# A two-layer graph network on one core: a wait, a GpSimd start and the last output block of the convolution are rearranged

## The reference

```python
src, dst = add_self_loops(edge_index, n)
h   = relu(gcn_conv(x1, W1, b1, src, dst, n))
out = gcn_conv(h, W2, b2, src, dst, n)
# gcn_conv(x, W, b): h = x @ W; dinv = 1/sqrt(deg); scatter-add of h[src]*dinv[src]*dinv[dst]; + b
return layernorm(x1 + out)      # (x - mean) / sqrt(var + 1e-5) over the 768 features
```

## Time and profile before

| | us |
|---|---|
| runs (median of 3) | 1649.15 |
| the profiled execution's own time | 1648.01 |
| its span in the profile | 1646.2 |
| TensorE busy in the span | 1624.3 |
| VectorE busy | 1222.6 |
| ScalarE busy | 761.0 |
| GpSimd busy | 217.7 |

### The profile page before, as it was taken

The page is one execution under the profiler, slowest core; times in us unless marked ns, Lnnn a source line. Parts: engine busy times, 40 slices in busy tenths (PEclk is TensorE's granted clock), DMA queues, the critical chain, the costliest instruction groups (busy, mean ns, idle before and its releaser), DMA issues. The chain is left out here.

```text
span 1646.2 us, 21875 instructions
## 1 busy us (share of the span) xinstructions
PE 1624.3 (99%) x7528; PEld 1360.4 (83%) x7528; DVE 1222.6 (74%) x2429; ACT 761.0 (46%) x1218; POOL 217.7 (13%) x145
## 2 busy tenths in 40 slices
PE   9999999999999999999999999999999998999998
PEld 6778888888878888888888888888888887989898
DVE  7778657655988778778777787887786668785447
ACT  3222223322565565556555555655565435644340
POOL 3112132222200000000000000000000001023003
PEclk9999999999999999999999999999999999999999
DMA  7444555984647475557647575865654447023222
GB/s 285 142 154 155 166 188 191 230 223 154 218 162 193 175 218 157 130 190 227 131 176 201 156 167 189 201 151 165 193 151 178 163 167 197 21 90 96 66 94 91
DMA packets 135396, 271.86 MB, mean 165 GB/s; under 512 B 24299, under 2 KB 83573, under 8 KB 122741
## 3 DMA queue, kind: packets, MB, share of 16 engines
q1 hardware_dynamic: 133844, 267.16, 53.6%
q0 software_dynamic: 1152, 3.15, 1.0%
q10 hardware_dynamic: 288, 0.13, 0.0%
HBM read 210.01 MB, written 60.40 MB: 164 GB/s over the span
## 5 line engine op out<-in xcount | busy, mean ns | idle before, releaser
L41 PE MATMUL psum<-ph,hc 128*128 128x512 f32 x768 | 299.3, 390 | 2.2 <-DVE pl L1079 1.2
L42 PE MATMUL psum<-pl,hc 128*128 128x512 f32 x768 | 298.8, 389 | 0.0
L43 PE MATMUL psum<-ph,hc 128*128 128x512 f32 x768 | 298.8, 389 | 0.0
L41 PE MATMUL psum<-wh,xTh 128*128 128x512 f32 x570 | 226.9, 398 | 0.7 <-issue 0.7
L42 PE MATMUL psum<-wl,xTh 128*128 128x512 f32 x570 | 222.4, 390 | 0.0
L43 PE MATMUL psum<-wh,xTl 128*128 128x512 f32 x570 | 222.3, 390 | 0.0
L1018 DVE CUSTOM_DVE_ANT_0 junk<-psum,a_bc 128x512 bf16<-128x512 f32 (+1 forms) x256 | 129.9, 554 | 115.7 <-ACT st L666 105.5
L666 ACT CAST st<-psum 128x512 fp32r<-128x512 f32 x96 | 56.4, 588 | 290.2 <-PE psum L43 287.4
L739 ACT ACTIVATE he<-mean,bias 128x512 f32<-128x512 f32 x96 | 69.6, 725 | 237.2 <-DVE mean L1167 237.2
L41 PEld LDWEIGHTS psum<-ph,hc 128*128 128x128 f32 x768 | 144.1, 188 | 33.9 <-DVE pl L1079 2.1
L43 PEld LDWEIGHTS psum<-ph,hc 128*128 128x128 f32 x768 | 144.1, 188 | 29.9
(11 more groups left out here) (292 smaller groups left out, 3162.0 us busy)
## 6 DMA issues: line engine op xcount, KB each, us to landing
hc<-h_scratch SPq DMA_DIRECT2D x96, 1024.0 KB, 6.1
h_scratch<-st SPq DMA_DIRECT2D x96, 512.0 KB, 3.2
w2r<-in_L_gnn_W SPq DMA_DIRECT2D x96, 384.0 KB, 7.0
wr<-in_L_gnn_W SPq DMA_DIRECT2D x11, 1536.0 KB, 9.1
gwr<-in_L_gnn_W SPq DMA_DIRECT2D x24, 384.0 KB, 3.4
row_bc<-logits_scratch SPq DMA_DIRECT2D x16, 512.0 KB, 13.7
expo_bc<-expo_scratch SPq DMA_DIRECT2D x16, 512.0 KB, 6.3
a_bc<-in_L_gnn_a_src SPq DMA_DIRECT2D x12, 256.0 KB, 7.0
```

The costliest lines, as they stand in the source:

```text
L41: nc.tensor.matmul(out, sh, mh, start=first, stop=False, skip_group_check=not grouped)
L42: nc.tensor.matmul(out, sh, ml, start=False, stop=False, skip_group_check=not grouped)
L43: return nc.tensor.matmul(out, sl, mh, start=False, stop=last, skip_group_check=not grouped)
```

## The change

1. TensorE: in the first group, the wait for `sx_lo` is left out at the last row block (b = 7), and stands instead ahead of the four low products of line 2120.
2. GpSimd: the counts of half 0 begin when `y_lo` has reached 6 (all low parts of the first product made), instead of when `sx_lo` has reached 8.
3. The last output block is split as 512 and 256 columns instead of 384 and 384, in TensorE's products, the additions and the stores. It is measured in three pieces of 256 columns. VectorE scales the 512 columns, ScalarE the 256 (`x * root + (-mean * root)`); for this VectorE writes the negated mean, and ScalarE multiplies it by the root.
4. Four more semaphores of the early part are cleared by GpSimd and used again.

```diff
-    early_sems = [edges_in, key_int, key_made, keyT_full, span_done, touch_full]
+    early_sems = [edges_in, key_int, key_made, keyT_full, span_done, touch_full, low_out, key_out, cols_full, cols_done]
...
+    END_PARTS = ((0, CW), (CW, D))
...
-        pool.wait_ge(sx_lo, NB)
+        pool.wait_ge(y_lo, FB)
...
-            act.wait_ge(norm_step, NORM_STEPS * n + NORM_ROOT)
+            act.wait_ge(norm_step, NORM_STEPS * n + (NORM_ROOT if n < NB - 1 else END_ROOT))
...
+        b, (lo, hi) = HNB - 1, END_PARTS[1]
+        act.wait_ge(norm_step, NORM_STEPS * (NB - 1) + END_ROOT + 2)
+        nc.scalar.activation(end_shift[:, 1:2], end_shift[:, 0:1], ACT.Copy, scale=root[:, b:b + 1]).then_inc(root_done, 1)
+        act.wait_ge(root_done, NB + 1)
+        nc.scalar.activation(x1[:, b, lo:hi], x1[:, b, lo:hi], ACT.Identity, bias=end_shift[:, 1:2], scale=root[:, b:b + 1]).then_inc(end_done[1], 1)
...
+            for j in range(lo // 256, hi // 256):
+                nc.vector.bn_stats(end_stats[:, j, :], x1[:, b, j * 256:(j + 1) * 256]).then_inc(norm_step, 1)
...
+        nc.vector.tensor_scalar(end_shift[:, 0:1], moments[:, b, 0:1], -1.0, None, ALU.mult).then_inc(norm_step, 1)
...
-        for i in range(2):
-            cs = slice(i * HC, (i + 1) * HC)
-            nc.vector.tensor_scalar(x1[:, b, cs], x1[:, b, cs], moments[:, b, 0:1], root[:, b:b + 1], ALU.subtract, ALU.mult).then_inc(norm_step, 1)
+        lo, hi = END_PARTS[0]
+        nc.vector.tensor_scalar(x1[:, b, lo:hi], x1[:, b, lo:hi], moments[:, b, 0:1], root[:, b:b + 1], ALU.subtract, ALU.mult).then_inc(end_done[0], 1)
...
                     pe.wait_ge(sx_hi, b + 1)
-                    pe.wait_ge(sx_lo, b + 1)
+                    if b < NB - 1:
+                        pe.wait_ge(sx_lo, b + 1)
...
+            pe.wait_ge(sx_lo, NB)
             for f in group:
                 nc.tensor.matmul(banks[f][:, :], xl[:, NB - 1, f * P:(f + 1) * P], ch[:, NB - 1, :], start=False, stop=True,
...
-                cs = slice(i * HC, (i + 1) * HC)
+                lo, hi = END_PARTS[i] if n == NB - 1 else (i * HC, (i + 1) * HC)
+                cs = slice(lo, hi)
```

More of the change, by code:

```diff
@@ L1801, in _ @@
             conv_tensor(pe, many_linked)
-NORM_STEPS, NORM_ROOT = 6, 4
+NORM_STEPS, NORM_ROOT, END_ROOT = 6, 4, 5
 def normalise(nc, dve, row, stats, moments, root, n, added, step, root_done):
@@ L1868, in graph_convolution @@
     root = put("groot", 100608, [P, NB], F32)
+    end_stats = put("gend_stats", 100640, [P, 3, 6], F32)
+    end_shift = put("gend_shift", 100736, [P, 2], F32)
+    END_PARTS = ((0, CW), (CW, D))
     ch2 = put("gch2", 102464, [P, NB, HALF], F32R)
@@ L1883, in graph_convolution @@
     agg_full, added, norm_step, root_done, out_done = (spare.pop() for _ in range(5))
+    end_done = [spare.pop() for _ in range(2)]
     CH = 2 * FB
@@ L1926, in sync @@
         b = HNB - 1
-        for i in range(2):
-            cs = slice(i * HC, (i + 1) * HC)
-            sp.wait_ge(norm_step, NORM_STEPS * NB + i)
-            sp.dma_start(out[b * P:(b + 1) * P, cs], x1[:, b, cs]).then_inc(out_done, 16)
+        for i, (lo, hi) in enumerate(END_PARTS):
+            sp.wait_ge(end_done[i], 1)
+            sp.dma_start(out[b * P:(b + 1) * P, lo:hi], x1[:, b, lo:hi]).then_inc(out_done, 16)
         sp.wait_ge(out_done, 16 * (NB + 1))
     def gpsimd(pool):
-        pool.wait_ge(sx_lo, NB)
+        pool.wait_ge(y_lo, FB)
         pool.wait_ge(ch_hi, NB)
@@ L2079, in vector @@
         dve.wait_ge(xb, NB)
-        for i in range(2):
-            cs = slice(i * HC, (i + 1) * HC)
+        for i, (lo, hi) in enumerate(END_PARTS):
             dve.wait_ge(agg_full, NB + i)
-            nc.vector.scalar_tensor_tensor(out=x1[:, b, cs], in0=banks[2 * (n % 4) + i][:, 0:HC], scalar=dinv[:, b:b + 1], in1=x1[:, b, cs],
+            nc.vector.scalar_tensor_tensor(out=x1[:, b, lo:hi], in0=banks[2 * (n % 4) + i][:, 0:hi - lo], scalar=dinv[:, b:b + 1], in1=x1[:, b, lo:hi],
                                            op0=ALU.mult, op1=ALU.add).then_inc(added, 1)
             dve.wait_ge(added, 2 * n + i + 1)
-            nc.vector.bn_stats(stats[:, b, i, :], x1[:, b, cs]).then_inc(norm_step, 1)
-        dve.wait_ge(norm_step, at + 2)
-        nc.vector.bn_aggr(moments[:, b, :], stats[:, b, :, :].rearrange("p i s -> p (i s)")).then_inc(norm_step, 1)
+            for j in range(lo // 256, hi // 256):
+                nc.vector.bn_stats(end_stats[:, j, :], x1[:, b, j * 256:(j + 1) * 256]).then_inc(norm_step, 1)
         dve.wait_ge(norm_step, at + 3)
+        nc.vector.bn_aggr(moments[:, b, :], end_stats[:, :, :].rearrange("p i s -> p (i s)")).then_inc(norm_step, 1)
+        dve.wait_ge(norm_step, at + 4)
         nc.vector.tensor_scalar(root[:, b:b + 1], moments[:, b, 1:2], LN_EPS, None, ALU.add).then_inc(norm_step, 1)
+        nc.vector.tensor_scalar(end_shift[:, 0:1], moments[:, b, 0:1], -1.0, None, ALU.mult).then_inc(norm_step, 1)
         dve.wait_ge(root_done, n + 1)
         nc.vector.reciprocal(root[:, b:b + 1], root[:, b:b + 1]).then_inc(norm_step, 1)
-        dve.wait_ge(norm_step, at + 5)
-        for i in range(2):
-            cs = slice(i * HC, (i + 1) * HC)
-            nc.vector.tensor_scalar(x1[:, b, cs], x1[:, b, cs], moments[:, b, 0:1], root[:, b:b + 1], ALU.subtract, ALU.mult).then_inc(norm_step, 1)
+        dve.wait_ge(norm_step, at + END_ROOT + 2)
+        lo, hi = END_PARTS[0]
+        nc.vector.tensor_scalar(x1[:, b, lo:hi], x1[:, b, lo:hi], moments[:, b, 0:1], root[:, b:b + 1], ALU.subtract, ALU.mult).then_inc(end_done[0], 1)
     def tensor(pe, many):
@@ L2198, in tensor @@
                         pe.wait_ge(rows_hi, s + 1 if s < HNB else HNB + 2 * (s - HNB) + 2)
-                    nc.tensor.matmul(bank[:, 0:HC], high[:, s, bs], xh[:, s, cs], start=(s == 0), stop=False)
+                    nc.tensor.matmul(bank[:, 0:hi - lo], high[:, s, bs], xh[:, s, cs], start=(s == 0), stop=False)
                 with pe.If(many > 0):
@@ L2202, in tensor @@
                     for s in range(NB):
-                        nc.tensor.matmul(bank[:, 0:HC], low[:, s, bs], xh[:, s, cs], start=False, stop=False)
+                        nc.tensor.matmul(bank[:, 0:hi - lo], low[:, s, bs], xh[:, s, cs], start=False, stop=False)
                 for s in range(NB):
@@ L2206, in tensor @@
                         pe.wait_ge(rows_lo, s + 1 if s < HNB else HNB + 2 * (s - HNB) + 2)
-                    last = nc.tensor.matmul(bank[:, 0:HC], high[:, s, bs], xl[:, s, cs], start=False, stop=(s == NB - 1))
+                    last = nc.tensor.matmul(bank[:, 0:hi - lo], high[:, s, bs], xl[:, s, cs], start=False, stop=(s == NB - 1))
                 if n == NB - 1 and i == 0:
```

## The result

Nine runs of the changed kernel have a median of 1653.49 us, nine of the kernel before 1649.15: ratio 1.0027, 95% interval 1.0018 to 1.0035. The change made the kernel slower by 4.3 us (0.26%). That is above the 0.2% that I had called no change, though the interval reaches down to 0.18%, and it is just outside the range. The profiled execution is the fastest of the nine (1651.35 us); its span is 1649.6 us, 3.4 more than before.

What follows compares the result with a forecast made beforehand. TensorE, busy 1624.3 of 1646.2 us, was taken as the bound; +2.1 us from the stall less 0.2 at the end gave +1.9, so 1649.9 for one execution and a median of 1651.0 us, range 1646.8 to 1653.2.

Steps and rivals of the forecast that it cites:

- What follows in PE's order is dense, and takes the delay over in full: TensorE after its stall for chunk 10: the delay of 2.1 us against before is kept whole.
- Rival A: GpSimd's counts keep their 24.26 us, `c0_lo` at 1507.8, TensorE +4.3 us, total 1653.2 us; chance 0.12.
- Part 1: Moved `sx_lo` wait at block 7: high products start before `sxl` is done, putting TensorE 0.97 us earlier.
- Part 2, the start: With GpSimd idle, VectorE is not slowed, so TensorE's step k = 1 starts 1.65 us sooner (bounds 1.5 and 1.8).
- The gap of 7 us moves with the first subtraction: GpSimd's 7.01 us of issue after its first cast belongs to the first subtraction and moves later with it.
- Rival B: No stall, because the 7.01 us gap does not move or GpSimd runs clean: 1647.3 us; chance 0.18.
- `c0_lo` at 1505.65: GpSimd's counts complete at 1505.65: first subtraction at 1483.57 plus 17.1 us of blocks and 5.0 us of slowing.
- The stall: TensorE waits 3.8 us for weight chunk 10, ready at 1518.0, and stands 2.1 us later than before.
- point of decision: `c0_lo` at 1501.9: each us the counts finish beyond it costs TensorE one us.
- Part 3: Last output block as 512 and 256 columns: TensorE's time unchanged, the end 0.2 us earlier (bounds 0 and 0.4).
- rival C: In the last block, 256 columns cost TensorE as much as 384, ending it 0.85 us later: 1651.9 us; chance 0.05.
- The median: Whole kernel: runs' median lies 1.14 us above the profiled-like execution's 1649.9, so 1651.0 us, +0.12%.

Runs made afterwards that it cites:

- e7: Changed kernel plus 28 extra TensorE products of 128 columns just before its wait for weight chunk 10 (result invalid, timing only): 1652.00 us, ratio 1.0022.
- e3: Kernel before with only TensorE's wait on the last `sxl` moved behind the high products, ahead of the low ones: 1647.85 us, ratio 0.9995.
- e5: Changed kernel, but ScalarE and VectorE make weight chunks 10 and 11 before the counts of half 1: 1646.31 us, ratio 0.9984.
- e6: Changed kernel plus one extra GpSimd subtraction of 128 columns at the counts' old starting point: 1645.71 us, ratio 0.9983.
- e1: Changed kernel, but GpSimd's counts start where they did before, at the last `sxl`: 1648.01 us, ratio 0.9995.
- e2: Kernel before with only GpSimd's counts started later, at `y_lo` 6: 1654.83 us, ratio 1.0033.
- e8: Changed kernel, but GpSimd's counts start at `y_lo` 3 instead of 6: 1646.49 us, ratio 0.9985.

## Why the prediction was wrong

**The step that failed** is "What follows in PE's order is dense, and takes the delay over in full". Dense it is, but not at the same speed: behind a stall of 4.5 us the clock was granted at half level for over 3 us (10 products of 0.32 us instead of 0.174, and what lies around them: 1.7 us by the yardstick, 1.4 to 1.6 by e7's profile). I had worked out a stall of 3.8 us and never asked what an idle TensorE costs when it is over. The prediction put this at nothing without a reason. In the convolution before, TensorE ran at 1.00 with no idle time above the 0.87 us of the earlier trace rows; but the same trace, at its start, had a row that shows the cost, and I did not look there. TensorE idles 2.94 us, the clock is then at 0.50, and products of 512 columns start 0.43 us apart (46.23, 46.66, 47.09) instead of 0.23. Timeline of PE, then windows, of the kernel before:
```profile
43.92 1.03 PE L1541 MATMUL psum<-hot_key,hot_low 128*128 128x256 bf16 x4 [2.94 <-issue]
...
46.66 0.63 PE L43 MATMUL psum<-wh,xTl 128*128 128x512 f32 x1
```
```profile
44.00:46.00 2.00, 1.81 (x8) 0.50 0.69 234
46.00:48.00 2.00, 2.00 (x7) 0.71 0.00 0
```
The sum for an execution was +1.9 us, and the yardstick shows +4.0: 0.6 for a later chunk 10 (+2.7 instead of +2.1), 1.7 for the slow clock, 0.1 for the end, less the 0.3 of the dense stretches. Without the clock's 1.7 the changed kernel would have stayed in the range. Rival A had nearly the right time (1653.2) for a wrong reason: by the yardstick the counts came 0.5 us later than forecast, and not 2.2.

Point by point:
- *Part 1, 0.97 us.* The low products of block 7 start 1.10 us after the `sxl`'s start instead of 2.16: 1.06, right. Alone it is worth 0.1 (e3): the whole gain is only there once the counts have left the stretch. I had the two parts as terms of one chain, but not that the first is nothing without the second.
- *Part 2, the start, 1.65 us in sum.* Step k = 1 starts 13.80 us from `sxl` (1476.26) instead of 15.59 (1478.64): 1.79, of which 1.38 is there at the end of step k = 0 (13.92 instead of 15.30) and the rest is the wait for chunk 1. In e5, 1.78 is left at the first `grows`. Right within its bounds.
- *The gap of 7 us moves with the first subtraction.* Right: 6.7 to 7.9 us in all thirteen traces where that subtraction follows its cast, and none in e6. Rival B's reason falls. What the gap is, loaded code as the prediction took it or something else, no run shows.
- *`c0_lo` at 1505.65.* It came at 1505.59, which is luck. Cast and gap took 8.96 instead of 7.62, the blocks 21.2 instead of 22.1, and the whole stretch began 0.59 us sooner. By the yardstick it is 43.13 instead of 42.60 us.
- *12.3 us from the counts to chunk 10.* 12.34, right.
- *The stall.* 3.8 forecast, 4.5 measured (1513.46 to 1517.98). Shown to be the cause by e1 and e2, to hang on the order and not on GpSimd's lateness by e5, with its point of decision met within 0.1 us by e6.
- *Part 3.* 256 columns take 0.114 us each ((1643.21 - 1642.30) / 8), half of 512 and a little under the line's 0.120; rival C falls. The tail gave 0.1 to 0.2 instead of 0.2: ScalarE's product of 128x1, whose scale is read from a tile, took 0.29 instead of 0.2.
- *The median.* The profiled execution before lay 1.14 us below its median; the one after (1651.35) 2.1 below. Its mean granted clock is 0.997, and that of seven of the other eight 0.991 to 0.995, so the slow clock may well cost the median more than the 1.7 us of its profile (not shown: they were not profiled, and the clock also falls in the attention layer). Reading sums off one execution leaves 1 to 2 us open in this kernel.

What stays open: how long the clock stays at half level after an idle time (3 us after a stall of 4.5, nearly 6 after 4.3 in e2, which is the wrong way round for a simple rule), what decides whether it falls at all (near 1372 the same idle time did both), and what makes the last output blocks differ by up to 0.8 us from trace to trace.

## What to carry to other kernels

An engine off the critical path has a deadline. Before its work is moved later, follow its semaphore to whoever waits, and then everything queued behind that waiting instruction: here weights that had nothing to do with the counts stood behind them. Before, the counts were complete 5.3 us before ScalarE asked for them (1496.01, 1501.27), and chunk 10 was ready 2.3 us before TensorE wanted it: 7.6 us of slack in all. By the yardstick the counts came 10.2 us later (43.13 instead of 32.96), and step k = 4 began 2.7 us later, the 2.6 that the slack did not hold. The cheapest cure was to let the urgent work pass first (e5), or to lay the idle start-up time of the helper over the stretch in which it disturbs (e8). A TensorE stall is to be priced as its length plus the slow products behind it; here a stall of 4.5 us cost 1.7 us more, and one of 4.3 in e2 2.9 more. To get such a price before the change is made, look through the whole trace of before for the nearest idle time of TensorE and read the rows behind it.

## What the hardware showed that was not expected

- GpSimd and VectorE are slower beside each other, GpSimd in steps: of the 112 subtractions of the counts in the fourteen traces 54 took 1.29 to 1.35 us, 17 took 1.63 to 1.66, 36 took 1.90 to 1.92, and five another time, up to 2.10. The same `gwl` on VectorE took 0.96 us alone and up to 2.07 beside GpSimd; moving TensorE 1 us ahead without moving GpSimd only shifted VectorE's work into more of it (e3).
- 28 products of 128 columns started 0.11 us apart (3.24 us in all), as 256 columns do (0.114): between 128 and 256 columns the width made no difference here.
- TensorE's clock fell or did not fall behind the same idle time of 1.6 us in the same code, in nine and five of fourteen profiled executions.
